# Cross-attention on one core: sums of exponentials by a transposing VectorE pass, a new order within a slot and shorter lags

## What is computed

```python
Q = split_heads(query @ Wq + bq)
K = split_heads(key @ Wk + bk)
V = split_heads(value @ Wv + bv)
scores = jnp.einsum('bhqd,bhkd->bhqk', Q, K) / np.sqrt(D_K).astype(np.float32)
attn = jax.nn.softmax(scores, axis=-1)
ctx = jnp.einsum('bhqk,bhkd->bhqd', attn, V)
out = ctx @ Wo + bo
return _layer_norm(out + query, ln_gamma, ln_beta)
```

## Time and profile before

| | us |
|---|---|
| median of three runs | 676.41 |
| the profiled execution's own time | 677.69 |
| its span, first to last instruction | 675.9 |
| TensorE matmul busy | 643.8 (95%) |
| VectorE busy | 555.0 (82%) |
| ScalarE busy | 319.7 (47%) |
| GpSimd busy | 453.7 (67%) |
| mean granted TensorE clock | 0.983 of 2.4 GHz |

### The profile page before, as it was taken

How to read it: one execution, slowest core, us unless ns; L and a number is a source line. 1 busy time by engine, 2 the same in 40 slices (tenths; PEclk the granted TensorE clock), 3 DMA queues, 4 the chain that set the end, 5 groups by cost and what they waited for, 6 DMA issues and landing times.

```text
span 675.9 us, 11503 instructions
## 1 busy us (share of the span) xinstructions
PE 643.8 (95%) x3336; PEld 435.1 (64%) x3336; DVE 555.0 (82%) x842; ACT 319.7 (47%) x547; POOL 453.7 (67%) x396
## 2 busy tenths in 40 slices
PE   6989997999999999999999999999999999999990
PEld 5978754666666666666666666666666666665570
DVE  5534484888889898888988888889888888988986
ACT  5612254545545555554555545455554544544431
POOL 0422143477777777777787777777877777666897
PEclk9999996999999999999999999999999999999996
DMA  9757788767776868778787778686767778675512
GB/s 318 288 198 186 193 203 208 179 162 199 194 201 170 209 180 205 204 195 215 201 197 184 201 186 204 190 201 186 198 177 206 198 205 215 152 185 154 162 62 93
DMA packets 105677, 129.55 MB, mean 192 GB/s; under 512 B 49936, under 2 KB 49936, under 8 KB 105648
## 3 DMA queue, kind: packets, MB, share of 16 engines
q1 hardware_dynamic: 105648, 129.19, 71.8%
HBM read 53.94 MB, written 24.35 MB: 116 GB/s over the span
## 4 chain that ended last, share of the span: by engine, by line
PE 77%; DVE 6%; SPq 6%; issue 2%; POOL 1%; DMA 1%; ACT 0%; POOLq 0%; DVEq 0%; ACTq 0%
PE p_q L584 24%; PE p_o L646 23%; PE p_s L614 9%; PE p_v L627 9%; PE p_d L630 7%; PE p_a L600 5%; SPq L519 3%; DVE rden L799 2%; SPq L505 1%; DMA xt<-in_x_t 1%; DVE cxt L813 1%; DVE stats L795 1%; DVE y L793 0%; POOL rstd L932 0%; DVE stats L887 0%
## 5 line engine op out<-in xcount | busy, mean ns | idle before, releaser
L799 DVE RECIPROCAL rden<-p_d 128x512 f32<-128x512 f32 x64 | 214.9, 3358 | 27.8 <-PE p_d L630 27.7
L709 ACT ACTIVATE prob<-p_s 77x512 f32<-77x512 f32 x256 | 144.0, 588 | 111.4 <-PE p_s L614 111.0
L834 DVE TENSOR_REDUCE nm<-p_a 128x4 f32<-128x308 f32 x256 | 117.4, 462 | 29.3 <-PE p_a L600 26.0
L936 POOL TENSOR_TENSOR y<-y,gamma_row 128x512 f32<-128x512 f32 x60 | 76.7, 1278 | 70.7 <-ACT y L739 70.7
L926 POOL TENSOR_TENSOR xl<-xt,xh 128x512 fp32r<-128x512 f32 x60 | 77.5, 1291 | 64.8 <-ACT xh L716 63.5
L584 PE MATMUL p_q<-xh,wqh 128*128 128x512 f32 x256 | 101.8, 398 | 1.7 <-PEq L148 1.7
L584 PE MATMUL p_q<-xl,wqh 128*128 128x512 f32 x256 | 101.8, 398 | 0.0
L584 PE MATMUL p_q<-xh,wql 128*128 128x512 f32 x256 | 101.1, 395 | 0.0
L945 POOL TENSOR_TENSOR cl<-cxt,ch 128x512 fp32r<-128x512 f32 x64 | 82.5, 1288 | 26.3 <-ACT ch L734 26.3
L739 ACT ACTIVATE y<-y,nmr,rstd 128x512 f32<-128x512 f32 x60 | 48.9, 815 | 106.1 <-DVE nmr L818 106.1
L614 PE MATMUL p_s<-z,ks 97*77 97x512 f32 x256 | 95.7, 414 | 0.0
(11 more groups left out here) (114 smaller groups left out, 911.8 us busy)
## 6 DMA issues: line engine op xcount, KB each, us to landing
z<-qh SPq DMA_DIRECT2D x256, 128.0 KB, 2.7
xt<-in_x_t SPq DMA_DIRECT2D x64, 256.0 KB, 2.8
z<-ql SPq DMA_DIRECT2D x128, 128.0 KB, 2.4
xn<-in_x SPq DMA_DIRECT2D x60, 256.0 KB, 3.1
out_dram<-y SPq DMA_DIRECT2D x60, 256.0 KB, 3.3
ks<-k_high SPq DMA_DIRECT2D x32, 154.0 KB, 3.5
cx<-in_ctx_t SPq DMA_DIRECT2D x4, 616.0 KB, 5.4
k_high<-kth SPq DMA_DIRECT2D x4, 616.0 KB, 3.5
```

Source lines behind the costliest of these rows:

```text
L709: nc.scalar.activation(prob[0:S2, j, :], p_s[j % 2][0:S2, :], ACT.Exp, scale=SCALE).then_inc(prob_ready, 1)
L799: nc.vector.reciprocal(rden[:], p_d[:]).then_inc(rden_ready, 1)
L834: nc.vector.tensor_reduce(nm[:, t, HC * (g.k % 2):HC * (g.k % 2 + 1)], p_a[t % 2][:, 0:HC * S2].rearrange("p (h k) -> p h k", k=S2), AX_X, ...
```

## The change

The ones matmuls into p_d go. VectorE instead sums over the keys with a reduction that transposes 32 x 32 blocks on the way (`sum_keys`, prob padded with zeros to 96 partitions), into a tile part of 96 partitions by 4 x 16; four tiny matmuls with a selection matrix sel (96 x 32, three identities, made by GpSimd at the start) add the three blocks of keys into p_den, 16 columns a head; VectorE takes the reciprocal of these 16 columns and spreads them by a block transpose of 128 x 512 into rden.

The order in a slot changes: TensorE does the whole projection of q first, then the values, two scores, and then the output projection with the other scores and the row maxima. The maxima of a chunk are made in the slot of its projection (LAG_ROWMAX goes). The first score comes two slots after the projection where it was four (LAG_SCORE), the values three where it was five, output and all that follows two slots sooner. SyncE issues z in the odd slot and the maxima in the even one, each a slot sooner.

```diff
-LAG_ROWMAX = 1
-LAG_PV = 5
-LAG_SCORE = 4
-LAG_OUT = 9
-LAG_NORM = 10
-LAG_SCALE = 11
-LAG_STORE = 12
+LAG_SCORE = 2
+LAG_PV = 3
+LAG_OUT = 7
+LAG_NORM = 8
+LAG_SCALE = 9
+LAG_STORE = 10
+WO_SLOTS = (3, 5)
...
-V_SLOTS = (0, 1, 1, 2, 3, 3)
+V_SLOTS = (0, 0, 1, 1, 2, 2)
...
             def slot(g):
-                if g.k % 2 == 1 and g.back(3).valid(NG):
-                    load_maxima(g.back(3))
                 if g.k % 2 == 0 and g.back(2).valid(NG):
-                    c = g.back(2)
+                    load_maxima(g.back(2))
+                if g.k % 2 == 1 and g.back(1).valid(NG):
+                    c = g.back(1)
...
-                if g.k % NCH == 1 and g.valid(NG):
-                    load_ks(g.back(1))
-                if g.k % NCH == 3 and g.valid(NG):
-                    load_v(g.back(3))
-                if g.k % NCH == NCH - 1 and g.back(-1).valid(NG):
+                if g.k % NCH == 0 and g.valid(NG):
+                    load_ks(g)
+                if g.k % NCH == 2 and g.valid(NG):
+                    load_v(g.back(2))
+                if g.k % NCH == 1 and g.back(1 - NCH).valid(NG):
...
+                pe.wait_ge(part_ready, g.over(1, 1))
+                at_least(pe, rec_ready, g.over(1))
                 for j in range(HC):
-                    last = nc.tensor.matmul(p_d[DK * j:DK * (j + 1), :], ones[0:S2, :], prob[0:S2, j, :],
+                    last = nc.tensor.matmul(p_den[DK * j:DK * (j + 1), 0:QB], sel[:], part[:, QB * j:QB * (j + 1)],
                                             start=True, stop=True)
...
+                s, v, o = g.back(LAG_SCORE), g.back(LAG_PV), g.back(LAG_OUT)
+                if g.valid(NG):
+                    for kc in range(KC):
+                        project_q(g, kc)
                 if v.valid(NG):
                     values(v)
                 if s.valid(NG):
                     scores(s, 0)
                     scores(s, 1)
...
+                for kc in range(KC):
+                    if o.valid(NS):
+                        project_out(o, kc)
+                    if s.valid(NG) and kc in (1, 2):
+                        scores(s, kc + 1)
+                    if g.valid(NG):
+                        rowmax_scores(g, kc)
...
             def slot(g):
                 s, v, m, n = g.back(LAG_SCORE), g.back(LAG_PV), g.back(LAG_NORM), g.back(LAG_SPLIT)
...
                 if n.valid(NG):
                     split_x_high(n)
...
                 if g.valid(NG):
                     q_high(g)
-                if s.valid(NG) and not short:
-                    exp(s, 3)
+                if s.valid(NG):
+                    for j in range(HC):
+                        exp(s, j)
...
+            def sum_keys(g):
+
+                dve.wait_ge(prob_ready, g.over(1, 1, HC))
+                at_least(dve, pv_summed, g.over(1))
+                nc.vector.tensor_reduce(part[:], prob[0:KP, :, :].rearrange("p h (i r) -> p (h i) r", r=DK),
+                                        AX_X, ALU.add, apply_transpose=True).then_inc(part_ready, 1)
+
             def invert_sums(g):
+
                 dve.wait_ge(pv_summed, g.over(1, 1))
-                nc.vector.reciprocal(rden[:], p_d[:]).then_inc(rden_ready, 1)
+                at_least(dve, rden_ready, g.over(1))
+                nc.vector.reciprocal(rec[:], p_den[:, 0:QB]).then_inc(rec_ready, 1)
+                dve.wait_ge(rec_ready, g.over(1, 1))
+                at_least(dve, cx_ready, g.over(1))
+                nc.vector.transpose(rden[:].rearrange("p (i r) -> p i r", r=DK),
+                                    rec[:].unsqueeze(2).broadcast_to([P, QB, DK])).then_inc(rden_ready, 1)
...
-                r, v, m = g.back(LAG_ROWMAX), g.back(LAG_PV), g.back(LAG_NORM)
+                v, m = g.back(LAG_PV), g.back(LAG_NORM)
+                if v.valid(NG):
+                    sum_keys(v)
                 if m.valid(NS):
                     add_residual(m)
                     dve.wait_ge(stats_ready, m.over(1, 1))
+                if g.valid(NG):
+                    q_low(g)
                 if v.valid(NG):
                     invert_sums(v)
...
                     divide(v)
                 if m.valid(NS):
                     variance(m)
...
+                if g.valid(NG):
+                    for t in range(QT):
+                        row_maxima(g, t)
+                    if g.k % 2 == 1:
+                        turn_maxima(g)
                 if m.valid(NS):
                     mean_over_std(m)
```

More of the change, by code:

```diff
@@ L33 @@
 HALF = 2 * HC
+KP = 3 * DK
 PAIR = 2 * NCH
@@ L270, in _ @@
                 nc.gpsimd.memset(keep["kb0"][:].bitcast(F32), 0.0).then_inc(keep["kb0_zeroed"], 1)
-                nc.gpsimd.memset(keep["ones"][:], 1.0)
                 nc.gpsimd.memset(keep["minus_half"][:], -0.5)
+                sel = keep["sel"]
+                nc.gpsimd.memset(sel[:], 0.0).then_inc(sel_ready, 1)
+                for b in range(KP // DK):
+                    pool.wait_ge(sel_ready, b + 1)
+                    nc.gpsimd.affine_select(out=sel[:], in_=sel[:], compare_op=ALU.not_equal, fill=1.0, base=-DK * b,
+                                            pattern=[[-1, DK]], channel_multiplier=1).then_inc(sel_ready, 1)
                 def x_low(n):
@@ L324, in attend @@
     KR = QI + 1
+    QB = S // DK
     wqh, wql, woh, wol, bq_col = (keep[n] for n in ("wqh", "wql", "woh", "wol", "bq_col"))
-    xt, xh, xl, y, ones, minus_half, bv_row = (
-        keep[n] for n in ("xt", "xh", "xl", "y", "ones", "minus_half", "bv_row"))
+    xt, xh, xl, y, sel, minus_half, bv_row = (
+        keep[n] for n in ("xt", "xh", "xl", "y", "sel", "minus_half", "bv_row"))
     ch, cl = keep["ch"], keep["cl"]
@@ L355, in attend @@
         prob = sb("prob", [P, HC, S], F32)
+        part = sb("part", [KP, HC * QB], F32)
+        rec = sb("rec", [P, QB], F32)
         rden = sb("rden", [P, S], F32)
@@ L362, in attend @@
         ve, rstd, nmr = (sb(n, [P, 4, 1], F32) for n in ("ve", "rstd", "nmr"))
-        p_q, p_v, p_d, p_o = (psum(n) for n in ("p_q", "p_v", "p_d", "p_o"))
+        p_q, p_v, p_den, p_o = (psum(n) for n in ("p_q", "p_v", "p_den", "p_o"))
         p_s = [psum(f"p_s{i}") for i in range(2)]
@@ L383, in attend @@
             sem(n) for n in ("wo_high", "qh_ready", "prob_ready", "ch_ready", "normed"))
-        max_turned = sem("max_turned")
+        max_turned, part_ready, rec_ready = (sem(n) for n in ("max_turned", "part_ready", "rec_ready"))
         ql_ready, max_ready, rden_ready, cx_ready, y_ready, stats_ready = (
@@ L425, in wo_in_slot @@
             for half in range(2):
-                if g.back(LAG_PV + 2 * half).is_first():
+                if g.back(WO_SLOTS[half]).is_first():
                     return [2 * half, 2 * half + 1]
@@ L549, in slot @@
                     store_v(i)
-                if g.back(LAG_PV).is_first():
+                if g.back(WO_SLOTS[0]).is_first():
                     for row, src in ((gamma, "ln_gamma"), (beta, "ln_beta"), (bo, "bo")):
                         sp.dma_start(row[:], a[src].partition_broadcast(P)).then_inc(rows_in, 16)
-                if g.back(LAG_PV + 1).is_first():
+                if g.back(WO_SLOTS[0] + 1).is_first():
                     load_wo(2)
@@ L707, in exp @@
                 if j == 0:
+                    if g.is_first():
+                        act.wait_ge(const_dve, 3)
                     at_least(act, pv_summed, g.over(1))
+                    at_least(act, part_ready, g.over(1))
                 nc.scalar.activation(prob[0:S2, j, :], p_s[j % 2][0:S2, :], ACT.Exp, scale=SCALE).then_inc(prob_ready, 1)
@@ L783, in _ @@
             nc.vector.memset(ks[QI:KR, :, :, :].bitcast(F32), 1.0).then_inc(const_dve, 1)
-            dve.wait_ge(const_dve, 2)
+            nc.vector.memset(prob[DK * 2:KP, :, :], 0.0).then_inc(const_dve, 1)
+            dve.wait_ge(const_dve, 3)
             dve.wait_ge(keep["bq_in"], 16)
@@ L978, in _ @@
             run(pool, slot)
+            add_bo_last(QT - 1)
             last = [Slot(0, NS + t) for t in range(-2, QT)]
```

22 lines of the change are left out of this document (6 added, 16 removed).

## The result

The changed kernel takes 980.4 us, median of four runs (978.81 to 980.98), against 676.47: 1.449 times the time before, 95% interval 1.446 to 1.451. The forecast was 956 in a range of 880 to 1020, slower at 0.94.

What follows compares the result with a forecast made beforehand. TensorE's matmul issue bounded the old kernel; after the change, SyncE's late transfers would. First score at 80, three pairs 80.5, 28 pairs of 26.9 (753) and 42.3 at the end give 956 us, range 880 to 1020.

Steps and rivals of the forecast that it cites:

- C: SyncE's chain from the odd chunk's ql to the even chunk's first score: 14.0 us, 16.1 with kb, mean 15.1.
- Sums of exponentials: New sums per slot: VectorE 3.27 us for 3.36, so no gain; TensorE's tiny matmuls 0.35 us for 0.86.
- D: Way from the even chunk's first score to the next odd chunk's ql, through TensorE and VectorE: 9.5 us.
- the clock: TensorE at half rate for some 5 us behind each pair's pause, losing 2.3 us, all in D.
- Pair: Period of two slots as a loop: 15.1 + 9.5 + 2.3 = 26.9 us, against 18.18 before.
- Start and end: First score at 80 us, first three pairs 80.5, and 42.3 from chunk 62's first score to the end.
- the three short pairs: First three pairs, without output projection and statistics but with other start work: 32 + 25 + 23.5 = 80.5 us.
- tail: From chunk 62's first score to the end of the kernel: 42.3 us, kept from the kernel before.
- Rival (1): SyncE's chain is on time and nothing waits: 8.7 us a slot, 652 us in all; chance 0.05.
- Rival (2): The stall comes but TensorE's clock stays at 2.4 GHz: 24.6 us a pair, 885 us; chance 0.15.
- Rival (3): Stall with low clock lasting 9 us and the transposing sum at 3.1 us: 1018 us; chance 0.2.
- The signs: Unbroken z, xt, xn, store, maxima on SyncE; TensorE idle 6 to 9 us; clock falling once a pair.

Runs made afterwards that it cites:

- the run with filled pauses: Changed kernel plus 28 overwritten 512-column matmuls ahead of each even chunk's first score, filling TensorE's pause: 926.7 us, ratio 1.368.
- the last run: Changed kernel, lags one slot longer, xt first and z last on SyncE, first reduction before product, mean over deviation with scalar operand: 654.2 us, ratio 0.965.
- the first experiment: Changed kernel with every lag one slot longer, nothing else: 869.0 us, ratio 1.284 to the kernel before.
- the third run with z last: Changed kernel, lags one slot longer, z behind all other SyncE transfers, first reduction before product, mean over deviation with scalar operand: 683.0 us, ratio 1.011.

## Why the prediction was right, step by step

- **C**, from ql to the first score: forecast 14.0 and 16.1 us, measured 13.92 (536.40 to 550.32) and 16.44 (506.73 to 523.17). Over the full pairs its mean is 15.2 (15.1). The landing of the maxima, taken as 2.0 from the rows of others, is 1.84 us from the start of the fourth issue in the chain.
- **Sums of exponentials**: the transposing sum 2.30 us (2.3), the reciprocal of 16 columns 0.25 (0.26), the transpose 0.71 (0.71), the tiny matmuls last 0.23 to 0.26 us a slot (0.35). VectorE's gain was nothing, as forecast, and TensorE's did not show, as it was not the bound.
- **D** was forecast as 9.5 and 2.3 for the clock, 11.8; measured 13.2 with kb (523.17 to 536.40) and 11.8 without (550.32 to 562.13), mean of the full pairs 12.5. This term was under-sized, by two errors that partly cancel. The mean over deviation, taken as 0.15 us like the other one-column rows, takes 1.1 us in the even slots, ahead of the transposing sum in D. That is the larger error: 9.5 and 0.95 make the 10.4 us that D has in the run with filled pauses. The low clock was over-sized: it held for 6.1 us behind the pause with kb and about 3 behind the other, and that run puts its price at 1.9 us a pair, not 2.3.
- **Pair**: 26.9 forecast; 28 pairs lie between the first scores of chunks 6 (161.07) and 62 (936.16), 27.7 us each. These 0.8 us a pair are 22 of the 24 us that the forecast was short.
- **Start and end**: first score at 80, measured 82.9; the three short pairs 80.5, measured 78.2 (82.92 to 161.07); tail 42.3, measured 43.0.
- **Rival (1)**, nothing late, was priced at 652 us. Its condition was not met, as z and the maxima were issued just as the earlier trace rows said. That the last run takes 654 is no test of that price: it has lags one slot longer, the first reduction ahead of the product and a shorter one-column row, and its slots are mostly 8.3 to 8.6 us where the rival had 8.7. **Rival (2)**, the clock kept, was priced at 885; with the pauses filled it is 927. Some 29 of these 42 us are the mean over deviation (0.95 us in 31 pairs, an estimate), which the rival's 24.6 us a pair lacked as well. **Rival (3)** was wrong in both of its terms: the low clock lasts 3 to 6 us, not 9, and the sum 2.30 us, not 3.1.
- **The signs**: z, xt, xn, store and maxima came in the order and without the breaks that were named, and the clock fell once a pair (mean 0.835, about 0.8 forecast). TensorE's busy share is 69% and VectorE's 59% (two thirds). SyncE's lines hold 31% of the chain, not half. The page names no releaser ("issue") ahead of the pauses without kb, as in the row at 550.32, so this share is a lower bound of SyncE's part.
- What the forecast did not say: the transfers behind z (xt in both slots, xn) form loops of their own, one behind the other. They lay hidden under the wait for the maxima, so the forecast of the change did not need them, while the expectation of the first experiment, one slot more and 655 us, did and was wrong by 214 us. Undoing the cause that binds uncovered three more of the same kind (xt of the odd slot, xn, xt of the even slot): 980, 869, 744, 697, 683, 654 us, of which the step from 697 to 683 is the two edits on VectorE.

Not tried: the z or maxima transfers issued from another engine, three buffers for z, the new sums in the old order, and the shorter one-column row in the old kernel. How the 11 us that the shorter row brought split between the row itself and the waits behind it was not separated.

## What to carry to other kernels

Before a stage is moved nearer to its source, walk the issuing queue in program order from the last input to the last landing; the sum of the issues (here twelve of 0.65 us) is a latency, though the queue has time to spare in every pair of slots. Then do the same for every transfer that stands behind the long group: each is late by the group's length, whoever needs it. Put the group whose inputs come last at the end of the queue's slot, and count a long pause of TensorE twice, as idle time and as slow matmuls behind it.

## What the runs showed of the hardware that was not expected

A one-column VectorE instruction can take nine times its time beside GpSimd. In the changed kernel, VectorE and GpSimd at the same moment:

```profile
501.21 1.11 DVE L828 SCALAR_TENSOR_TENSOR nmr<-mv,rstd 128x1 f32<-128x1 f32 x1
```

```profile
501.01 1.29 POOL L948 TENSOR_TENSOR cl<-cxt,ch 128x512 fp32r<-128x512 f32 x1 [5.40 <-ACT ch L741]
```

It ends at 502.32, as GpSimd's does at 502.30; ten microseconds later (511.24), with no GpSimd instruction beside it, the same line takes 0.12. In the whole kernel 31 of its 62 instances last over 0.5 us, and each of these ends within 0.03 us of the end of a GpSimd instruction that had started before it. By the kernel's text it is VectorE's only instruction in a slot that reads two tensors in SBUF. Over the kernel its duration ranges from 116 to 1245 ns; with the deviation as a scalar operand (the third run with z last) it is 170 to 214 in every case:

```profile
L828 DVE SCALAR_TENSOR_TENSOR nmr<-mv,rstd x62: 116/356/1245, 167.4 to 968.0; 128x1 f32<-128x1 f32 x62
```

```profile
L828 DVE TENSOR_SCALAR nmr<-mv,rstd x62: 170/203/214, 148.4 to 666.8; 128x1 f32<-128x1 f32 x62
```

(The Trainium skill, page SBUF — State Buffer, section "SBUF: two separate sides", has a VectorE instruction with two SBUF inputs and a GpSimd instruction that reads SBUF share a port pair by an exclusive lock, held for the whole instruction by whichever starts first. Both rows agree.)
